# Cross-attention in a decoder layer: the eight PSUM banks dealt out anew, and the order of the projections, the mask and the input loads moved

## Chip, cores and metric

One core of a Trainium2 chip runs the whole kernel. The metric is the device time of one execution in microseconds (us). PE is TensorE, DVE is VectorE, ACT is ScalarE, POOL is GpSimd, SP is SyncE (it only issues DMAs here); PEld is the weight load of PE.

## What is computed

A decoder layer on x of shape (8, 512, 512): self-attention with 16 heads of 64, then cross-attention with 16 heads of 32 to a context of (8, 512, 384) with a key mask, then a quantised feed-forward; each with a layer norm in front and a residual. The change touches only the cross-attention:

```python
q = (x @ Wq) ...; k = (context @ Wk) ...; v = (context @ Wv) ...   # 16 heads of 32
scores = einsum('bhid,bhjd->bhij', q, k) * 32 ** -0.5
scores = where(context_mask[:, None, None, :], scores, max_neg)
out = einsum('bhij,bhjd->bhid', softmax(scores, -1), v)
return x + out @ Wo
```

## The kernel before

All of it is in `cross_attention_and_feed_forward_stage`, written by hand: each engine has its own instruction stream and waits on semaphores.

**Order.** The work goes by groups and slots. A group n is 4 heads of one batch element (4 groups to a batch element, N = 32 in all), and a slot is one tile of 128 keys by 512 queries of one head, so a group has U = 16 slots. Every engine walks the same list (G, s, t): G counts slots, s = G // 16 is the group whose scores are being made, t = G % 16. In slot G, PE issues, in this order: the scores of tile G-8 into bank `st` (`scores`, L2562), the maximum product of tile G+14 into `mx` (`max_scores`, L2544), at t = 3 the four transposes of the maxima into `ms` (`max_rows`, L2554), its share of the projections for group s+2, and the product with the values of tile G-12 into `ov` (`product`, L2572). Each product in float32 is made of parts: a value is split into a high and a low part, so a projection is three passes over its weights.

**Projections.** `KPASS` and `QPASS` (L1237) say how many matmuls of `key_projection` (9, L2514) and `query_projection` (12, L2525) a slot gets: keys 3 each in slots 0 to 2, queries 3 each in slots 3 to 6. Values (9 matmuls a tile, four tiles to a batch element) come in slots 7 to 10 and 12 to 15 of three groups out of four. A slot with a projection is called full here, one without is light. In the groups with s % 4 = 1 there are no values, but four tiles of context are transposed.

**Banks.** Keys go to `pj[:, 0]`, queries to `pj[:, 1]`, and every head's product goes to the one bank `ov`. `product` waits at the first tile of each head until ACT has copied the last head out (`out_rows`, L1918, which writes `osb`, first thing in its slot). Each key projection waits for `masked_key` of the group before, each query projection for `low_query` of the group before.

**Splitting.** DVE multiplies the keys by the mask (`masked_key`, L2105, in slot 3 behind the maximum and the two steps of the exponents), ACT takes the high part (`high_key`, slot 4), POOL the low part (`low_key`, slot 5). Queries: `high_query` on ACT in slot 7 (L1888), `low_query` on DVE in slot 8 (L2112). DVE also takes a maximum per slot (`maxima`, L2124) and half of the low parts of the exponents; POOL has the other half.

**SP.** It has no clock: it goes down its list and waits where a semaphore is not there yet. `stack_keys` and `stack_queries` (L1637, L1650; t = 8) send the seven 256 KB pieces of keys and queries to the tiles that PE reads; they wait for all scores of group n-3. `max_rows` (L1657, t = 5) sends the row of maxima that the first scores of the group need in slot 8. `outputs` (L1662, t = 1, 5, 9, 13) stores a head: `c_raw` (64 rows by 512, seen as 2 by 32 by 512) and `c_sums`. In groups with s % 4 = 1 there are also `load_sums` (L1670, t = 2, waits until all heads of the last batch element have landed; DVE takes their reciprocals in slot 5), `load_x` high (L1622, t = 7), `load_mask` (L1628, t = 9), `load_x` low (t = 9), and `store_reciprocals` (t = 10).

**Output projection.** From G = 474 on, `out_work` is mixed in every four slots, and goes on alone after the last slot. Its accumulators `acc` are `mx[:, 0]` and `pj[:, 1]`, its transposes `pt` go to `mx[:, 1]` and `ms`, and `spread_reciprocals` (L2612) writes `pj[:, 0]`.

Of the kernel before, what the change touches and what calls it, by code (L numbers as in the profile page):

```python
# [1215 lines left out]
def cross_attention_and_feed_forward_stage(nc, env):  # L1216
# [20 lines left out]
    KPASS, QPASS = (3, 3, 3), (0, 0, 0, 3, 3, 3, 3)  # L1237
# [33 lines left out]
    with ExitStack() as ctx:  # L1271
# [4 lines left out]
        with ExitStack() as life:  # L1276
# [51 lines left out]
            pj = bank("pj", [P, 2, S])  # L1328
            st = bank("st", [P, 2, S])
            mx = bank("mx", [P, 2, S])  # L1330
            ov = bank("ov", [P, S])
            ms = bank("ms", [P, S])
        dve_q = su.sem("dve_q")
# [197 lines left out]
        acc = lambda j: pj[:, 1] if j % 2 else mx[:, 0]  # L1531
        pt = lambda j: ms if j % 2 else mx[:, 1]
# [83 lines left out]
        def _(e):  # L1616
# [193 lines left out]
            for G, s, t in slots():  # L1810
                n = s + 2
                if t == 7 and s >= 0 and s % XG == 1 and s // XG + 1 < B:
                    load_x(s // XG + 1, 0)
                if t == 5 and 0 <= s < N:
                    max_rows(s)
                if t == 8 and n < N:
                    stack_keys(n)
                    stack_queries(n)
                if t == 1 and s >= 0 and s % XG == 0 and s // XG + 1 < B:
                    for i in range(NT):  # L1820
                        load_context(NT * (s // XG + 1) + i)
                if t % NT == 1 and 0 < s:
                    outputs(s - 1, t // NT)
                if t == 9 and s >= 0 and s % XG == 1 and s // XG + 1 < B:
                    load_mask(s // XG + 1)
# [50 lines left out]
        def _(e):  # L1876
# [11 lines left out]
            def high_query(n):  # L1888
                e.wait_ge(pe_q, n + 1)
                nc.scalar.activation(qh[:, :], pj[:, 1], ACT.Copy).then_inc(act_qh, 1)  # L1890
# [27 lines left out]
            def out_rows(n, j):  # L1918
# [3 lines left out]
                nc.scalar.activation(osb[:, j], ov[0:VW, :], ACT.Copy).then_inc(act_ov, 1)  # L1922
# [70 lines left out]
            for G, s, t in slots():  # L1993
# [21 lines left out]
                if t == 7 and n < N:  # L2015
                    high_query(n)
# [81 lines left out]
        def _(e):  # L2098
# [6 lines left out]
            def masked_key(n):  # L2105
# [4 lines left out]
                nc.vector.tensor_tensor(km[:, :], pj[:, 0], maskb[:, :], ALU.mult).then_inc(dve_km, 1)  # L2110

            def low_query(n):  # L2112
# [3 lines left out]
                nc.vector.tensor_tensor(ql[:, :], pj[:, 1], f32(qh[:, :]), ALU.subtract).then_inc(dve_ql, 1)  # L2116
# [78 lines left out]
            def out_work(i):  # L2195
# [17 lines left out]
                if is_chunk(n):  # L2213
                    e.wait_ge(pool_o, n + 1)
                    e.wait_ge(pe_rb, n + 1)
                    nc.vector.tensor_tensor(osum[:, n % SUM], osum[:, n % SUM], pj[:, 0], ALU.mult).then_inc(dve_o, 1)
# [28 lines left out]
            for G, s, t in slots():  # L2245
                n = s + 2
                m = G + U - LM - 1
                if 0 <= m < U * N:
                    maxima(m)
                if t == 11 and value_tile(s, 0) is not None:  # L2250
# [10 lines left out]
                if t == 3 and n < N:  # L2261
                    masked_key(n)
                if t == 8 and n < N:
# [228 lines left out]
        def _(e):  # L2492
# [21 lines left out]
            def key_projection(n):  # L2514
# [3 lines left out]
                if n:  # L2518
                    e.wait_ge(dve_km, n)
                for i, (w, part) in enumerate(((w_hi, 0), (w_lo, 0), (w_hi, 1))):  # L2520
                    for k in range(CK):
                        yield nc.tensor.matmul(pj[:, 0], w[:, k, cols(n % XG)], xc[:, part, k],  # L2522
                                               start=(i == 0 and k == 0), stop=(i == 2 and k == CK - 1))
# [297 lines left out]
```

## Time and profile before

| | us |
|---|---|
| median of 3 runs | 3456.7 |
| lowest, highest | 3453.31, 3459.38 |
| the profiled execution, its own time | 3453.76 |
| its span | 3452.1 |
| busy: PE, DVE, ACT, POOL | 3188.3, 2610.2, 2258.7, 1102.8 |
| cross-attention, first key projection to the end of the output projection | about 1544 to 2506 |

"Busy" of an engine counts its instructions; a matmul's duration overlaps the next one's start, so an engine can look busy through short waits. A wait stands in brackets behind the instruction that waited, with who released it. The DMA share is the mean over the 16 DMA engines. A window of the trace says, after its two ends: its length in us; the busy us of PE, PEld, DVE, ACT and POOL, each with its instructions in brackets; the granted PE clock as a share of full speed; the DMA share; GB/s, reads and writes together. The windows by batch element run from slot 3 of one s % 4 = 1 group to the next.

### The profile page before, as it was taken

Reading aid. Unit: us, or ns where it says so; the run is one execution under the profiler, and the core shown is the slowest. Engines: PE = TensorE matmul, PEld = TensorE weight load, DVE = VectorE, ACT = ScalarE, POOL = GpSimd, SP = SyncE. Lnnn points to the kernel's source line nnn. Section 1 sums busy time; section 2 is a strip of 40 time slices with the busy share of each in tenths; the row PEclk is TensorE's granted clock in tenths of the full one; section 3 lists DMA queues with packets and bytes.
Section 4 is the critical chain, followed back from the end, with each engine's and each line's share of the span. In section 5 each row is a group of like instructions: output and inputs, shape, how many; then the busy total and the mean of one; then the engine's idle time right before and its main releaser. Section 6 shows DMA issues by size and latency. Waiting matters only on the chain.

```text
span 3452.1 us, 47184 instructions
## 1 busy us (share of the span) xinstructions
PE 3188.3 (92%) x15056; PEld 2506.6 (73%) x15056; DVE 2610.2 (76%) x4327; ACT 2258.7 (65%) x4127; POOL 1102.8 (32%) x1192
## 2 busy tenths in 40 slices
PE   5999999999999999978999999988899999942998
PEld 4788888888888888865666666655678888731887
DVE  5987878787778777767888888887863479888564
ACT  4886767676766767655777777775442256578665
POOL 1233242333333333344666666666400000000000
PEclk9999999999999999989999999999999999975999
DMA  3453444444434433346656666555623268989764
GB/s 123 158 169 120 129 143 125 134 124 143 121 134 138 138 116 123 110 131 122 125 107 117 131 119 128 116 112 185 210 83 113 108 231 292 339 338 406 262 239 176
DMA packets 273028, 555.49 MB, mean 161 GB/s; under 512 B 28024, under 2 KB 105856, under 8 KB 259472
## 3 DMA queue, kind: packets, MB, share of 16 engines
q1 hardware_dynamic: 268560, 544.08, 52.6%
q10 hardware_dynamic: 4224, 8.39, 0.6%
q8 instruction: 124, 2.03, 0.2%
q14 instruction: 120, 0.98, 0.1%
HBM read 322.72 MB, written 162.30 MB: 141 GB/s over the span
## 4 chain that ended last, share of the span: by engine, by line
PE 37%; DMA 8%; DVE 5%; issue 2%; ACT 2%; SPq 1%; POOL 1%; POOLq 0%; ACTq 0%; DVEq 0%
PE gu_acc L2637 9%; PE ca_mx L2551 3%; PE ca_ov L2581 3%; PE md_acc L2723 3%; PE md_acc L2724 3%; PE md_acc L2725 3%; DMA ca_q<-ca_ql 2%; PE ca_ov L2582 2%; PE ca_st L2569 2%; PE ca_pj L2533 2%; PE ca_ms L2541 2%; PE ca_pj L2522 2%; DMA gu_g<-gate 1%; DMA gu_w_raw<-in_L_ffn_w_up_dram 1%; DMA md_ab<-up 1%
## 5 line engine op out<-in xcount | busy, mean ns | idle before, releaser
L915 POOL TENSOR_SCALAR sa_ex<-sa_ex,sa_rs 128x512 f32<-128x512 f32 x512 | 357.0, 697 | 906.6 <-DVE sa_rs L741 906.6
L736 DVE TENSOR_REDUCE sa_nm<-sa_st 128x1 f32<-128x512 f32 x512 | 350.3, 684 | 223.5 <-PE sa_st L1057 219.8
L578 ACT ACTIVATE sa_eh<-sa_tr 128x512 fp32r<-128x512 f32 x512 | 306.6, 599 | 293.5 <-PE sa_tr L1067 291.7
L1008 PE MATMUL sa_pj<-sa_xh,sa_w 128*128 128x512 f32 x1536 | 456.0, 416 | 3.0 <-DVE sa_xl L714 1.5
L2127 DVE TENSOR_REDUCE ca_negm<-ca_mx 128x1 fp32r<-128x512 f32 x512 | 345.0, 682 | 77.1 <-PE ca_mx L2551 74.8
L745 DVE TENSOR_TENSOR sa_el<-sa_tr,sa_eh 128x512 fp32r<-128x512 f32 x512 | 351.2, 686 | 41.0 <-ACT sa_eh L578 34.1
L571 ACT ACTIVATE sa_ex<-sa_st,sa_nm 128x512 f32<-128x512 f32 x512 | 351.3, 686 | 43.4 <-DVE sa_nm L736 39.5
L2420 POOL TENSOR_TENSOR ca_el<-ca_ex,ca_eh 128x512 fp32r<-128x512 f32 x256 | 359.9, 1411 | 40.0 <-ACT ca_eh L1916 39.1
L1908 ACT ACTIVATE ca_ex<-ca_st 128x512 f32<-128x512 f32 x512 | 298.5, 586 | 56.2 <-PE ca_st L2569 56.0
L1067 PE MATMUL sa_tr<-top_ident,sa_ex 128*128 128x128 f32 x2048 | 306.8, 272 | 1.9 <-POOL sa_ex L915 1.9
L1067 PEld LDWEIGHTS sa_tr<-top_ident,sa_ex 128*128 128x128 f32 x2048 | 254.3, 140 | 70.9 <-POOL sa_ex L915 4.3
L1008 PEld LDWEIGHTS sa_pj<-sa_xh,sa_w 128*128 128x128 f32 x1536 | 262.5, 190 | 40.5 <-issue 4.6
L1945 ACT ACTIVATE gu_ev<-gu_acc,top_x_scale 128x512 f32<-128x512 f32 x192 | 131.0, 683 | 203.7 <-PE gu_acc L2637 196.1
L1916 ACT ACTIVATE ca_eh<-ca_ex 128x512 fp32r<-128x512 f32 x320 | 201.3, 629 | 90.9 <-PE ca_ov L2582 86.8
L2142 DVE TENSOR_TENSOR ca_el<-ca_ex,ca_eh 128x512 fp32r<-128x512 f32 x256 | 247.4, 966 | 15.1 <-ACT ca_eh L1916 14.0
L2581 PE MATMUL ca_ov<-ca_eh,ca_vc 128*66 128x512 f32 x512 | 208.9, 408 | 27.3 <-ACT ca_osb L1922 22.7
L2551 PE MATMUL ca_mx<-ca_k,ca_q 97*128 97x512 f32 x512 | 212.3, 415 | 18.1 <-DMA ca_q<-ca_ql 14.3
L1008 PE MATMUL sa_pj<-sa_xl,sa_w 128*128 128x512 f32 x768 | 228.1, 405 | 0.0
L1078 PE MATMUL sa_ov<-sa_eh,sa_va 128*128 128x512 f32 x512 | 212.9, 416 | 4.2 <-DVE sa_el L745 3.6
L2569 PE MATMUL ca_st<-ca_q,ca_k 98*128 98x512 f32 x512 | 207.4, 405 | 5.8 <-DMA ca_q<-ca_mrow 5.8
L1056 PE MATMUL sa_st<-sa_ks,sa_qs 128*128 128x512 f32 x512 | 206.3, 403 | 0.0
L2582 PE MATMUL ca_ov<-ca_el,ca_vc 128*66 128x512 f32 x512 | 204.8, 400 | 0.0
(309 smaller groups left out, 7574.5 us busy)
## 6 DMA issues: line engine op xcount, KB each, us to landing
sa_w<-w_split SPq DMA_DIRECT2D x56, 1536.0 KB, 7.4
gate<-gu_ev SPq DMA_DIRECT2D x24, 1024.0 KB, 4.4
gu_g<-gate SPq DMA_DIRECT2D x48, 512.0 KB, 6.4
gate<-gu_g SPq DMA_DIRECT2D x48, 512.0 KB, 3.7
up<-gu_ev SPq DMA_DIRECT2D x24, 1024.0 KB, 5.7
md_ab<-gate SPq DMA_DIRECT2D x96, 256.0 KB, 6.5
md_ab<-up SPq DMA_DIRECT2D x96, 256.0 KB, 7.1
md_ab<-gate SPq DMA_DIRECT2D x44, 512.0 KB, 12.2
```

Of the source, the lines that this page charges most:

```text
L571: nc.scalar.activation(ex[:, u % U], st[:, u % 2], ACT.Exp, bias=nm[:, u % U:u % U + 1], accum_out=sums[:, u % U:u % U + 1]).then_inc(act_ ...
L578: nc.scalar.activation(eh[:, v % ER], tr[:, v % 2], ACT.Copy).then_inc(act_eh, 1)
L736: nc.vector.tensor_reduce(nm[:, u % U:u % U + 1], st[:, u % 2], AX_X, ALU.max, negate=True).then_inc(dve_mx, 1)
L745: nc.vector.tensor_tensor(el[:, v % ER], tr[:, v % 2], f32(eh[:, v % ER]), ALU.subtract).then_inc(dve_el, 1)
L915: nc.gpsimd.tensor_scalar(ex[:, u % U], ex[:, u % U], rs[:, u % U:u % U + 1], 1.0, ALU.mult, ALU.mult).then_inc(pool_n, 1)
L1008: yield nc.tensor.matmul(pj[:, bank], w[:, n % 2, m, part, k], xx[b % 2][:, k], start=(i == 0 and k == 0), stop=(i == 2 and k == DK - 1))
L1067: last = nc.tensor.transpose(tr[:, v % 2, rows(qt)], ex[:, (first + qt) % U, rows(kt)], ident[:, :])
L2127: nc.vector.tensor_reduce(negm[:, n % 2, qt, h:h + 1], mx[:, m % 2], AX_X, ALU.max, negate=True).then_inc(dve_mx, 1)
L2420: nc.gpsimd.tensor_tensor(el[:, a % EL], ex[:, a % EX], f32(eh[:, a % EL]), ALU.subtract).then_inc(low_done["pool"], 1)
L2551: nc.tensor.matmul(mx[:, m % 2], q4[0:MR + 1, r, h, cols(qt)], k4[0:MR + 1, r, h], start=True, stop=True).then_inc(pe_mx, 1)
L2581: nc.tensor.matmul(ov[0:VW, :], values, eh[:, a % EL], start=(kt == 0), stop=False)
L2637: last = nc.tensor.matmul(u_acc[:, a % BANKS], ww[:, k], xx[:, b, k], start=(n == 0 and k == 0), stop=(n == 2 and k == DK - 1))
```

## The change

It deals out the eight PSUM banks anew (`pj` one bank for keys, then queries; `ov` two banks, `ov[h % 2]`), and moves steps in the lists of PE, DVE, ACT and SP. Keys and queries now take turns in one bank: the query projection starts in slot 4 and waits for `masked_key` of its own group, the key projection waits for `low_query` of the group before. `product` waits for the head before last. `masked_key` stands right behind the maximum in slot 3.

```diff
-    KPASS, QPASS = (3, 3, 3), (0, 0, 0, 3, 3, 3, 3)
+    KPASS, QPASS = (3, 3, 3), (0, 0, 0, 0, 3, 3, 3, 3)
...
-            pj = bank("pj", [P, 2, S])
+            pj = bank("pj", [P, S])
+            ov0 = bank("ov0", [P, S])
             st = bank("st", [P, 2, S])
             mx = bank("mx", [P, 2, S])
-            ov = bank("ov", [P, S])
+            ov1 = bank("ov1", [P, S])
             ms = bank("ms", [P, S])
+            ov = (ov0, ov1)
...
-        acc = lambda j: pj[:, 1] if j % 2 else mx[:, 0]
-        pt = lambda j: ms if j % 2 else mx[:, 1]
+        acc = lambda j: ms[:, :] if j % 2 else mx[:, 0]
+        pt = lambda j: ov0 if j % 2 else mx[:, 1]
...
-                if t == 7 and s >= 0 and s % XG == 1 and s // XG + 1 < B:
+                if t == 10 and s >= 0 and s % XG == 1 and s // XG + 1 < B:
                     load_x(s // XG + 1, 0)
                 if t == 5 and 0 <= s < N:
                     max_rows(s)
                 if t == 8 and n < N:
                     stack_keys(n)
+                if t == 9 and n < N:
                     stack_queries(n)
+                if t == 4 and s >= 0 and s % XG == 1 and s // XG + 1 < B:
+                    load_mask(s // XG + 1)
...
-                if t == 9 and s >= 0 and s % XG == 1 and s // XG + 1 < B:
-                    load_mask(s // XG + 1)
+                if t == 12 and s >= 0 and s % XG == 1 and s // XG + 1 < B:
                     load_x(s // XG + 1, 1)
...
-                if t == 7 and n < N:
+                if t == 8 and n < N:
                     high_query(n)
...
+                if t == 3 and n < N:
+                    masked_key(n)
...
-                if t == 3 and n < N:
-                    masked_key(n)
-                if t == 8 and n < N:
+                if t == 9 and n < N:
                     low_query(n)
...
             def key_projection(n):
                 if n:
-                    e.wait_ge(dve_km, n)
+                    e.wait_ge(dve_ql, n)
...
             def query_projection(n):
-                if n:
-                    e.wait_ge(dve_ql, n)
+                e.wait_ge(dve_km, n + 1)
...
             def product(a):
                 if kt == 0:
                     e.wait_ge(dve_vl, NT * b + NT)
-                    if a:
-                        e.wait_ge(act_ov, a // NT)
+                    if a >= 2 * NT:
+                        e.wait_ge(act_ov, a // NT - 1)
-                nc.tensor.matmul(ov[0:VW, :], values, eh[:, a % EL], start=(kt == 0), stop=False)
+                nc.tensor.matmul(ov[h % 2][0:VW, :], values, eh[:, a % EL], start=(kt == 0), stop=False)
...
-                    if t == 3:
+                    if t == 4:
                         work["q"] = query_projection(n)
```

In the output projection, tile 1 now waits for `ms` (`bank_free`) at its product, and for the last head in `ov0` at its transposes; `spread_reciprocals` and the DVE step behind it use all of `pj`.

## Rows read from the trace of the kernel before

**Rows 1.** Windows: length; busy PE, PEld, DVE, ACT, POOL; clock; DMA share; GB/s.
```profile
1698.56:1796.71 98.15, 94.45 (x405) 66.20 (x404) 81.56 (x123) 75.34 (x142) 60.11 (x53) 0.98 0.63 121
...
1893.43:1988.99 95.56, 92.89 (x405) 65.18 (x404) 82.12 (x123) 75.00 (x142) 60.45 (x53) 1.00 0.64 124
...
2183.24:2281.87 98.63, 94.97 (x405) 66.20 (x404) 82.73 (x123) 75.41 (x142) 60.09 (x53) 0.98 0.60 112
```
**Rows 2.** Waits of PE, 1698.56 to 2281.87: who for whom, us in total, times, longest.
```profile
PE ca_ov L2581 <- ACT ca_osb L1922: 8.9, 20, 0.9
PE ca_st L2569 <- DMA ca_q<-ca_mrow: 5.8, 5, 1.8
PE ca_mx L2551 <- DMA ca_q<-ca_ql: 3.9, 5, 1.6
```
**Rows 3.** Groups of instructions of the page (section 5), DVE's two costly ones.
```profile
L2127 DVE TENSOR_REDUCE ca_negm<-ca_mx 128x1 fp32r<-128x512 f32 x512 | 345.0, 682 | 77.1 <-PE ca_mx L2551 74.8
L2142 DVE TENSOR_TENSOR ca_el<-ca_ex,ca_eh 128x512 fp32r<-128x512 f32 x256 | 247.4, 966 | 15.1 <-ACT ca_eh L1916 14.0
```
**Rows 4.** Timeline of PE: start, us, instruction.
```profile
1996.93 0.40 PE L2569 MATMUL ca_st<-ca_q,ca_k 98*128 98x512 f32 x1
...
2004.29 0.40 PE L2569 MATMUL ca_st<-ca_q,ca_k 98*128 98x512 f32 x1
...
2005.25 0.39 PE L2569 MATMUL ca_st<-ca_q,ca_k 98*128 98x512 f32 x1
...
2012.91 0.50 PE L2551 MATMUL ca_mx<-ca_k,ca_q 97*128 97x512 f32 x1 [1.64 <-DMA ca_q<-ca_ql]
```
**Rows 5.** Windows of 1 us: first group, three of the fastest batch element, the slowest.
```profile
1604.00:1605.00 1.00, 1.00 (x6) 0.73 (x5) 1.00 (x3) 1.00 (x3) 0.46 (x1) 1.00 0.00 0
...
1913.00:1914.00 1.00, 1.00 (x6) 0.71 (x5) 1.00 (x2) 0.90 (x3) 1.00 (x1) 1.00 1.03 203
...
1949.00:1950.00 1.00, 1.00 (x6) 0.78 (x5) 0.86 (x2) 1.00 (x3) 1.00 (x1) 1.00 0.10 31
1966.00:1967.00 1.00, 1.00 (x7) 0.72 (x6) 1.00 (x3) 0.61 (x2) 0.80 (x1) 1.00 0.13 49
...
2237.00:2238.00 1.00, 1.00 (x6) 0.81 (x5) 0.66 (x2) 1.00 (x3) 0.06 (x1) 1.00 0.03 10
```
**Rows 6.** The chain that ended last, 2060 to 2100: start, us, what.
```profile
2077.43 11.83 DMA c_sums<-ca_osb
2089.39 2.54 DMA ca_sums<-c_sums
2091.96 0.55 DVE ca_rec L2149
```
**Rows 7.** Timeline of SP (DMA issues): start, us to issue.
```profile
1992.38 0.66 SPq L1659 DMA_DIRECT2D ca_q<-ca_mrow  x1
...
1995.40 0.58 SPq L1625 DMA_DIRECT2D ca_xq<-xn_hi  x1
...
2000.65 0.75 SPq L1634 DMA_DIRECT2D ca_q<-ca_ql  x1
```
**Rows 8.** The mask tile: its DMAs from issue to landing.
```profile
DMA to landing us min/median/max: 3.2/11.7/12.4
```
**Rows 9.** Timeline of DVE around a masked key with s % 4 = 2.
```profile
2207.51 0.94 DVE L2142 TENSOR_TENSOR ca_el<-ca_ex,ca_eh 128x512 fp32r<-128x512 f32 x1
2209.23 0.69 DVE L2110 TENSOR_TENSOR ca_km<-ca_pj,ca_maskb 128x512 f32<-128x512 f32 x1 [0.79 <-issue]
```
**Rows 10.** Timeline of PE in the same group: the query pass of slot 4.
```profile
2210.26 0.40 PE L2533 MATMUL ca_pj<-ca_xq,ca_w_hi 128*128 128x512 f32 x1
```
**Rows 11.** Window behind the 1.80 us wait of 2217.60.
```profile
2217.60:2225.00 7.40, 7.40 (x25) 5.24 (x26) 5.20 (x7) 4.54 (x9) 3.58 (x3) 0.77 1.07 142
```
**Rows 12.** Waits, 2308 to 2400, and the longest one of ACT before them.
```profile
PE ca_ov L2581 <- ACT ca_osb L1922: 11.1, 11, 6.5
...
ACT ca_wo_hi L1968 <- DMA ca_xn<-in_L_xattn_Wo_dram: 8.4, 1, 8.4
```

More of the change, by code:

```diff
@@ L1889, in high_query @@
                 e.wait_ge(pe_q, n + 1)
-                nc.scalar.activation(qh[:, :], pj[:, 1], ACT.Copy).then_inc(act_qh, 1)
+                nc.scalar.activation(qh[:, :], pj[:, :], ACT.Copy).then_inc(act_qh, 1)
             def high_value(j):
@@ L1921, in out_rows @@
                     e.wait_ge(o_out[j], 32 * n)
-                nc.scalar.activation(osb[:, j], ov[0:VW, :], ACT.Copy).then_inc(act_ov, 1)
+                nc.scalar.activation(osb[:, j], ov[j % 2][0:VW, :], ACT.Copy).then_inc(act_ov, 1)
             def high_reciprocals(b):
@@ L2109, in masked_key @@
                     e.wait_ge(pool_kl, n)
-                nc.vector.tensor_tensor(km[:, :], pj[:, 0], maskb[:, :], ALU.mult).then_inc(dve_km, 1)
+                nc.vector.tensor_tensor(km[:, :], pj[:, :], maskb[:, :], ALU.mult).then_inc(dve_km, 1)
             def low_query(n):
@@ L2115, in low_query @@
                     e.wait_ge(stacked[(n - 1) % RING], STACKS * ((n - 1) // RING) + STACKS)
-                nc.vector.tensor_tensor(ql[:, :], pj[:, 1], f32(qh[:, :]), ALU.subtract).then_inc(dve_ql, 1)
+                nc.vector.tensor_tensor(ql[:, :], pj[:, :], f32(qh[:, :]), ALU.subtract).then_inc(dve_ql, 1)
             def low_value(j):
@@ L2215, in out_work @@
                     e.wait_ge(pe_rb, n + 1)
-                    nc.vector.tensor_tensor(osum[:, n % SUM], osum[:, n % SUM], pj[:, 0], ALU.mult).then_inc(dve_o, 1)
+                    nc.vector.tensor_tensor(osum[:, n % SUM], osum[:, n % SUM], pj[:, :], ALU.mult).then_inc(dve_o, 1)
                 j = i - 1
@@ L2518, in key_projection @@
                 if n:
-                    e.wait_ge(dve_km, n)
+                    e.wait_ge(dve_ql, n)
                 for i, (w, part) in enumerate(((w_hi, 0), (w_lo, 0), (w_hi, 1))):
                     for k in range(CK):
-                        yield nc.tensor.matmul(pj[:, 0], w[:, k, cols(n % XG)], xc[:, part, k],
+                        yield nc.tensor.matmul(pj[:, :], w[:, k, cols(n % XG)], xc[:, part, k],
                                                start=(i == 0 and k == 0), stop=(i == 2 and k == CK - 1))
@@ L2532, in query_projection @@
                     for k in range(DK):
-                        yield nc.tensor.matmul(pj[:, 1], w[:, 2 * CK + k, cols(g)], xq[:, part, k],
+                        yield nc.tensor.matmul(pj[:, :], w[:, 2 * CK + k, cols(g)], xq[:, part, k],
                                                start=(i == 0 and k == 0), stop=(i == 2 and k == DK - 1))
@@ L2577, in product @@
                     e.wait_ge(dve_vl, NT * b + NT)
-                    if a:
-                        e.wait_ge(act_ov, a // NT)
+                    if a >= 2 * NT:
+                        e.wait_ge(act_ov, a // NT - 1)
                 values = vc[b % 2][:, kt, HS * g + h]
-                nc.tensor.matmul(ov[0:VW, :], values, eh[:, a % EL], start=(kt == 0), stop=False)
-                nc.tensor.matmul(ov[0:VW, :], values, el[:, a % EL], start=False, stop=(kt == NT - 1)).then_inc(pe_av, 1)
+                nc.tensor.matmul(ov[h % 2][0:VW, :], values, eh[:, a % EL], start=(kt == 0), stop=False)
+                nc.tensor.matmul(ov[h % 2][0:VW, :], values, el[:, a % EL], start=False, stop=(kt == NT - 1)).then_inc(pe_av, 1)
             def out_product(i):
@@ L2588, in out_product @@
                     e.wait_ge(dve_mx, U * N)
+                if i == 1:
+                    bank_free()
                 if i >= 2:
@@ L2606, in out_transposes @@
                 elif j == 1:
-                    bank_free()
+                    e.wait_ge(act_ov, HS * N - 1)
                 for k in range(DK):
@@ L2618, in spread_reciprocals @@
                     e.wait_ge(dve_ql, N)
-                nc.tensor.matmul(pj[:, 0], cast_r[:, :], rc[:, n % 2], start=True, stop=True).then_inc(pe_rb, 1)
+                nc.tensor.matmul(pj[:, :], cast_r[:, :], rc[:, n % 2], start=True, stop=True).then_inc(pe_rb, 1)
             def u_transposes(i):
```

## The prediction

> **What bounds the kernel now.** I read the windows by batch element first. A batch element is four groups, 64 slots; the six from 1698.56 to 2281.87 take 583.3 us, 97.2 each, between 95.56 and 98.63 for the same instructions [rows 1]. The reader is to see two things: PE is busy 93 of 96 us in the fastest, so little can be had from PE; and they differ by 3 us with nothing different to compute, so something else holds them.
>
> Next the waits of PE [rows 2]. In six batch elements it waited 8.9 us for ACT to empty the bank of the last head (20 times, 0.45 on average), 3.9 for the last piece of the stacked queries, 5.8 for the row of maxima. In sum 18.6, 3.1 per batch element. Waits under about 0.16 do not show, since a matmul's 0.39 outlasts its pitch of 0.23 (a light slot of four matmuls: 2004.29 to 2005.25, 0.96) [rows 4].
>
> Third, who else is full. In a light slot DVE owes a maximum, 0.68, and half a low part, 0.97 / 2 = 0.48 [rows 3]: 1.16 at least against PE's 0.96. So light stretches go at DVE's pace already, and a wait of PE inside one is partly time it would have waited anyway.
>
> Last, the DMA engines, and here I see the bound. In 96 windows of 1 us over the fastest batch element the share is near 1 while the seven stack pieces run, and otherwise about 0.13; it never falls below 0.10 [rows 5]. 0.13 of 16 engines is two engines. Between the bursts exactly two are busy, without a hole, and the stores of the heads are what SP issues then. The two slowest batch elements have holes (0.03 at 2237). The chain agrees: a store of sums took 11.83 us to land, SP could not load the sums before, and DVE stood until the load had landed, 2.54 more [rows 6]. Once per batch element everything queued on those two engines has to be through.
>
> The Trainium skill, "DMA: Bandwidth & Descriptors", section on why a DMA increments its semaphore by 16, says that a DMA runs on the largest number of engines up to 16 that divides the slowest dimension of both sides, and on the lowest-numbered ones. By that rule a store seen as 2 by 32 by 512 runs on two engines, always the same; the share of 0.13 agrees.
>
> **Two banks for the heads.** This takes away the wait for `out_rows`. Ceiling: 8.9 us in six batch elements, 1.5 each, and a hidden 0.16 for each of 16 heads, 2.5. Floor: nothing, where DVE is late next. ACT's copies and their number stay. In steady state what remains is set by the two engines, below.
>
> **One bank for keys and queries.** No matmul is added. The query passes move from slots 3 to 6 to slots 4 to 7. Slot 3 keeps the four transposes and gets light, slot 7 gets full (six matmuls where values start too). PE's sum is the same, and DVE gains a full slot before the light ones: between 0 and 0.5 us per batch element, part of the next sum.
> The new wait for the masked key: in the tightest kind of group the key was masked from 2209.23 to 2209.92, after 0.79 us of a wait that is not named, which I read as the mask not landed [rows 9]. The new first query pass would stand where slot 4's pass is, less the 0.7 us that slot 3 loses: 2210.26 - 0.7 = 2209.6 [rows 10]. With the mask there early and the key ahead of the low part (0.94), it ends near 2208.8, 0.8 us ahead. Bounds: 0 per group, and 0.3 (2209.92 less 2209.6) if the mask were still late; I take 0. Behind `masked_key` on DVE stand two exponent steps, late by 0.68, which the full slot 4 covers; without cover POOL's and PE's next product would wait 0.68. The key projection's new wait is for a step of slot 9, seven slots earlier: 0.
> `high_query` and `low_query` come a slot later, 1 to 1.6 us. The queue hides it, because the four key pieces go out first and keep all engines busy. At the very start of the stage nothing hides it: +1 us once, at most 2.
>
> **The loads.** The high half of x (1 MB, issued 1995.40) goes behind the stack pieces instead of ahead, and `ql` (issued 2000.65, waited for until 2012.91 [rows 4, 7]) lands earlier by what 1 MB takes. At the 203 GB/s of the burst [rows 5] that is 5 us, or 10 if reads and writes share the figure; both are over the longest wait, 1.6. The 3.9 us go: 0.65 per batch element. But the row of maxima, two groups of stores later, waits for all of it in any order, so this wait moves to it. The low half of x is needed three slots after the high half and still lands before two stores that stand ahead of that row: 0.
> The mask (256 KB) leaves the burst for a quiet time: 1/16 of the 4 MB that are sent from 1995.40 on. Of the 17.5 us to 2012.91 that is 1.1; as the two engines have stores besides, I take half, 0.5 us less for the row of maxima; bounds 0 and 1.1. It now stands ahead of the row of maxima of the s % 4 = 1 group: issue 0.35, and data. That row is issued 1992.38 and needed 1996.93, 4.55 later [rows 4, 7]. Bounds: 0 and 3.2, a mask's shortest landing [rows 8]; I take 0.5, as most of 3.2 is latency that overlaps.
>
> **The sum, steady state.** PE's way gets shorter by up to 1.5 + 0.65 + 0.5, some 2.6 us per batch element; the mask gives 0.5 and takes 0.5. The two engines have the same bytes to move. They were full for 95.6 us in the fastest batch element, and holes are all that can be closed: 97.2 to some 96.4. So 0.8 in each of six, 5 us; the other 1.8 comes back as longer waits for the row of maxima and for the sums. **Before 1698** the engines have holes (a share of 0.00 at 1604 [rows 5]), so PE sets the pace and most of one batch element's 2.6 is won: -2, with the +1 at the start -1. **After 2308**: 11.1 us of waits for the head's bank, of which 6.5 lie behind ACT's 8.4 us wait for an output weight [rows 12], which blocks the exponents too and stays; of the other 4.6 I take half, as DVE and POOL are near full: -2. The banks of the output projection: 0. In all -8 us: the profiled execution 3453.76 to 3446, and, as it lies 2.9 below the median, 3449 against 3456.7; I say 3448.
>
> **Rivals.**
> *A. The two engines keep the pace* (above): 3448, own range 3442 to 3454. For it: a share that never falls under two engines. Against: that could be chance, with a backlog that just happens not to run out. Chance 0.45.
> *B. PE's waits set the pace.* Then 8.9 and 3.9 and 2 of the 5.8 are won in six batch elements, 14.8; as much per batch element before 1698, 2.5; 4.6 at the end: 22 us, 3435. For it: PE is 97% busy (92.89 of 95.56). Against: rows 1 and 6. Chance 0.22.
> *C. The banks' wait is only replaced by DVE's, no gain:* 3456. For it: 1.16 against 0.96 per light slot. Chance 0.13.
> *D. Slower: the mask ahead of the row of maxima.* It decides if that row takes over 4.55 us to land. With 2 us in each of seven batch elements, +14, less 5 of the rest: +9, 3466. A pause of 1.80 us also left PE at a granted clock of 0.77 for 7.4 us, which is 1.7 us lost [rows 11]; part of these would come on top. Chance 0.20.
> The Trainium skill, "DMA: Bandwidth & Descriptors", section "Queues, rings and completion order", says that each engine consumes its ring in order. By that a small row waits for the mask's packets ahead of it; it speaks for D, and no run here shows its price yet.
>
> **The numbers.** A measurement can tell about 0.2%, 7 us, from no change. Of A somewhat more than half lies beyond it (0.27), with all of B (0.22) and a bit of C: faster 0.51. Same: the rest of A and C and a little of D, 0.31. Slower 0.18. The range takes in B and nearly D: 3431 to 3465.
>
> **What would show it.** Right: no wait of PE for `ca_osb` of 0.3 to 0.9 between 1698 and 2281; no wait for `ca_ql` in s % 4 = 2; longer waits for `ca_mrow` and of SP for `c_sums`; batch elements of 96 to 97 us, the DMA share never under 0.10. If batch elements fall to 94, the two engines were no bound and I am wrong towards B. Waits for `ca_mrow` in s % 4 = 1 show D; waits of PE for `ca_km` would show the bank for keys and queries too tight.

## The result, and the profile after

| | before | after |
|---|---|---|
| median of 19 runs each, us | 3454.7 (3446.74 to 3465.61) | 3462.01 (3458.65 to 3468.17) |
| span of the profiled execution, us | 3452.1 | 3460.7 |

The ratio is 1.0018, with a 95% interval of 1.0011 to 1.0024. The changed kernel is slower by 0.18%. That is small, but the interval lies wholly on the slower side, where the forecast of 3448 had it faster.

The page of the changed kernel: the span, the row of busy times, and four groups of section 5. Where the head's product had waited for ACT, PE now waits for the row of maxima and for the maximum of DVE.

```profile
span 3460.7 us, 47184 instructions
...
PE 3188.3 (92%) x15056; PEld 2508.9 (72%) x15056; DVE 2616.6 (76%) x4327; ACT 2253.6 (65%) x4127; POOL 1097.9 (32%) x1192
...
L2131 DVE TENSOR_REDUCE ca_negm<-ca_mx 128x1 fp32r<-128x512 f32 x512 | 342.9, 680 | 85.5 <-PE ca_mx L2554 83.1
...
L2146 DVE TENSOR_TENSOR ca_el<-ca_ex,ca_eh 128x512 fp32r<-128x512 f32 x256 | 240.2, 938 | 17.5 <-ACT ca_eh L1920 16.4
L2554 PE MATMUL ca_mx<-ca_k,ca_q 97*128 97x512 f32 x512 | 213.4, 417 | 20.8 <-DVE ca_negm L2131 9.7
...
L2572 PE MATMUL ca_st<-ca_q,ca_k 98*128 98x512 f32 x512 | 209.2, 409 | 19.6 <-DMA ca_q<-ca_mrow 13.4
```

The waits of PE in the six batch elements, 1698.91 to 2290.11, the lines that answer to [rows 2]:

```profile
PE ca_st L2572 <- DMA ca_q<-ca_mrow: 11.8, 6, 2.1
PE ca_mx L2554 <- DVE ca_negm L2131: 7.1, 18, 0.5
PE ca_pj L2536 <- DMA ca_xq<-xn_hi: 3.8, 6, 0.8
PE ca_ms L2514 <- DVE ca_xc L2106: 1.5, 6, 0.3
```

The waits for `ca_osb` (8.9 us) and `ca_ql` (3.9) are gone, as meant. The one for the row of maxima doubled, from 5.8 to 11.8, and falls in every batch element; two are new, for DVE's maximum (before: 1.2) and for the high half of x.

Windows of the changed kernel by batch element, columns as in [rows 1]; three of the six; the first takes 97.44, the other five 98.65 to 98.97:

```profile
1698.91:1796.35 97.44, 93.12 (x405) 65.51 (x404) 83.05 (x123) 74.95 (x142) 60.05 (x53) 1.00 0.65 121
...
1895.00:1993.65 98.65, 94.39 (x405) 66.61 (x404) 83.58 (x123) 75.00 (x142) 59.56 (x53) 0.98 0.65 120
...
2191.43:2290.11 98.68, 94.45 (x405) 66.61 (x404) 83.34 (x123) 75.02 (x142) 59.38 (x53) 0.98 0.63 112
```

The six take 591.2 us against 583.3: +7.9. With +0.35 ahead of them (1698.91 against 1698.56) and +0.35 behind (+1.1 in the tail of the table below, -0.7 in the feed-forward), that is the 8.6 by which the spans differ. So the question is what happens inside a batch element, and there one cuts further: from slot 3 of each group (its transposes) to slot 3 of the next. The same batch element of the changed kernel in four windows, for the steps from s % 4 = 1 to 2, 2 to 3, 3 to 0 and 0 to 1:

```profile
1895.00:1918.67 23.67, 22.78 (x103) 15.52 (x102) 21.13 (x35) 19.41 (x39) 15.16 (x14) 1.00 0.78 149
1918.67:1945.36 26.69, 24.19 (x99) 17.07 (x98) 20.64 (x30) 18.54 (x35) 14.46 (x14) 0.94 0.58 121
1945.36:1969.59 24.23, 24.23 (x108) 18.01 (x107) 20.76 (x31) 18.78 (x36) 14.91 (x14) 1.00 0.68 116
1969.59:1993.65 24.06, 23.20 (x99) 16.00 (x98) 21.05 (x30) 18.26 (x35) 15.02 (x14) 1.00 0.57 93
```

and of the kernel before, its fastest batch element:

```profile
1893.43:1917.88 24.45, 23.16 (x102) 15.30 (x101) 20.33 (x35) 19.54 (x39) 15.55 (x14) 1.00 0.73 184
1917.88:1941.42 23.54, 22.64 (x100) 16.06 (x99) 20.85 (x30) 18.19 (x35) 14.94 (x13) 1.00 0.57 95
1941.42:1965.71 24.29, 24.29 (x109) 17.91 (x108) 20.90 (x31) 18.92 (x36) 14.85 (x14) 1.00 0.68 119
1965.71:1988.99 23.28, 22.81 (x99) 15.91 (x98) 20.03 (x30) 18.34 (x35) 15.10 (x14) 1.00 0.58 95
```

Summed over the six batch elements, for every kernel of this study (us; the tail runs from slot 3 of the last batch element's s % 4 = 1 group to the first matmul of the feed-forward):

| kernel | 1 to 2 | 2 to 3 | 3 to 0 | 0 to 1 | sum | tail |
|---|---|---|---|---|---|---|
| before | 151.1 | 146.3 | 145.9 | 140.0 | 583.3 | 224.3 |
| after | 142.0 | 159.4 | 145.5 | 144.3 | 591.2 | 225.4 |
| after_late | 143.3 | 149.0 | 145.5 | 144.3 | 582.0 | 232.6 |
| before_late | 179.8 | 144.7 | 146.1 | 139.9 | 610.5 | 235.7 |
| after_split | 142.0 | 139.9 | 145.5 | 144.3 | 571.6 | 219.4 |
| before_split | 151.1 | 141.2 | 145.9 | 140.2 | 578.4 | 216.8 |
| after_x7 | 162.5 | 141.7 | 145.5 | 144.2 | 593.9 | 222.1 |
| after_mask9 | 142.1 | 161.7 | 145.5 | 144.3 | 593.6 | 226.9 |
| as_onebank | 142.0 | 139.3 | 145.6 | 139.6 | 566.4 | 218.4 |
| as_kmlast | 143.5 | 140.7 | 146.8 | 145.6 | 576.5 | 218.6 |
| after_onebank | 142.6 | 157.2 | 148.0 | 139.4 | 587.2 | 221.9 |
| as_pause | 141.9 | 139.5 | 145.5 | 139.3 | 566.2 | 217.4 |
| bs_loads | 144.3 | 145.8 | 146.0 | 140.4 | 576.4 | 221.5 |
| after_fill | 142.0 | 153.3 | 145.5 | 144.3 | 585.0 | 224.5 |

The first two lines say it: the change wins 9.1 in the first step and loses 13.1 in the second and 4.3 in the fourth. The first loss holds the waits for the row of maxima (6.0 more) and for x (3.8). A third part shows in the windows right behind the wait for the row of maxima. Two of these waits in the timeline of PE of the changed kernel:

```profile
1732.75 0.50 PE L2572 MATMUL ca_st<-ca_q,ca_k 98*128 98x512 f32 x1 [1.82 <-DMA ca_q<-ca_mrow]
...
2027.61 0.50 PE L2572 MATMUL ca_st<-ca_q,ca_k 98*128 98x512 f32 x1 [2.06 <-DMA ca_q<-ca_mrow]
```

and the windows that begin at the ends of the first four:

```profile
1732.75:1740.00 7.25, 7.23 (x30) 4.89 (x30) 6.48 (x10) 5.89 (x11) 3.57 (x3) 1.00 1.09 148
1830.14:1838.00 7.86, 7.86 (x27) 5.58 (x28) 6.17 (x9) 5.49 (x11) 3.58 (x3) 0.78 1.09 146
1928.80:1936.00 7.20, 7.20 (x24) 5.05 (x25) 5.63 (x9) 4.81 (x9) 3.36 (x3) 0.76 1.07 147
2027.61:2035.00 7.39, 7.39 (x25) 5.24 (x26) 5.99 (x9) 4.89 (x10) 3.19 (x3) 0.77 1.08 151
```

Behind the pause of 1.82 us PE kept its full clock; behind the next three it ran at a mean of 0.76 to 0.78 of full speed, a mix of its two levels, 1.2 and 2.4 GHz. Of the six only the first batch element is spared, and it is the one of 97.44: 1.2 us shorter, of which 0.2 is its shorter wait. In the trace of the kernel before, the windows behind the waits of 1.65 and 1.80 us for the row of maxima stand at 0.77, those behind 1.41 and 0.73, and behind the 1.64 for the queries [rows 4], at 1.00: two falls there, five here. The three more, at 1.2 (the price that `after_fill` shows below), are about the rest of the 13.1 (6.0 + 3.8 + 3.7 = 13.5).

### The profile page after: what moved, and what is told of

It is laid out like the page before. It is cut to its first block, busy times and chain, and to the rows that moved or that the text cites. A ratio compares the mean times of both kernels' runs of the same rounds, so it can differ in the third digit from the quotient of the medians.

```text
span 3460.7 us, 47184 instructions
## 1 busy us (share of the span) xinstructions
PE 3188.3 (92%) x15056; PEld 2508.9 (72%) x15056; DVE 2616.6 (76%) x4327; ACT 2253.6 (65%) x4127; POOL 1097.9 (32%) x1192
## 4 chain that ended last, share of the span: by engine, by line
PE 34%; DVE 8%; DMA 8%; issue 2%; ACT 2%; SPq 1%; POOL 1%; ACTq 0%; POOLq 0%; DVEq 0%
PE gu_acc L2642 7%; PE ca_mx L2554 3%; PE md_acc L2728 3%; PE md_acc L2729 3%; PE md_acc L2730 3%; PE ca_st L2572 2%; PE ca_ov L2585 2%; PE ca_ov L2584 2%; DMA gu_g<-gate 2%; PE ca_pj L2536 2%; PE ca_pj L2526 2%; PE ca_ms L2544 2%; DMA ca_q<-ca_mrow 2%; DVE ca_negm L2131 1%; DMA gu_w_raw<-in_L_ffn_w_up_dram 1%
## 5 line engine op out<-in xcount | busy, mean ns | idle before, releaser
L2146 DVE TENSOR_TENSOR ca_el<-ca_ex,ca_eh 128x512 fp32r<-128x512 f32 x256 | 240.2, 938 | 17.5 <-ACT ca_eh L1920 16.4
```

## The experiments

Labels that begin with `after` or `before` change that kernel; `as_` stands on `after_split`, `bs_` on `before_split`. Each batch of runs has its own runs of the kernel before beside it, so kernels of different batches are compared by their ratios to it.

### Later stores: after_late, before_late

The first head's store goes behind the row of maxima.

```diff
-                if t % NT == 1 and 0 < s:
-                    outputs(s - 1, t // NT)
+                if t in (5, 6, 9, 13) and 0 < s:
+                    outputs(s - 1, 0 if t == 6 else t // NT)
```

> The changed kernel with one store moved: the first head's store (and sums) of the group before goes out in slot 6, behind the row of maxima, instead of in slot 1 ahead of it. Nothing is left out. Theory T1 (the row of maxima queues behind the stores of heads, which only two DMA engines carry; the pause of 2.05 us also costs PE its full clock): the row waits for two stores instead of three, so PE's wait for it, 2.05 us at s % 4 = 2, falls below 0.3, its clock stays at 1.00 in the window behind it, batch elements fall from 98.7 to about 96, and the kernel gains 12 to 20 us on the changed one. Theory T2 (the row waits for the x loads and stack pieces on all sixteen engines, whatever the stores do): the wait stays at 1.8 to 2.1 us and the time within 3 us. Theory T3 (the loss of the change comes from DVE, which falls behind in the light slots): waits for the row matter little, under 5 us gained.

> The same single move of one store in the kernel before. T1: its waits for the row (5 in six batch elements, 5.8 us) go, those for the queries (3.9) stay or grow a little; 3 to 8 us faster than before. T2 and T3: the same time within 3 us.

Measured: `after_late` 3465.66 us, ratio 1.0031 (1.002 to 1.0042). The wait for the row of maxima is gone, the one for the high half of x is 7.7 us in place of 3.8, and the batch elements take 97.0 instead of 98.5 on average. But the tail grew by 7.2 us, so in sum nothing was won, and the 12 to 20 us that T1 had expected did not come. In the tail, PE's waits for the reciprocals that the output projection loads (`ca_rc`) grew from 7.9 to 14.1 us; that the late stores make them is argued, not shown. What the run shows is that the row of maxima was late because of what SP sends ahead of it: with one head's store (and its sums) behind it the wait is gone.

`before_late` 3496.43 us, ratio 1.0118 (1.0104 to 1.0133), where T1 had it 3 to 8 us faster and the other two theories the same. Its wait for a DMA in 1698 to 2290:

```profile
PE ca_mx L2551 <- DMA ca_q<-ca_ql: 23.7, 6, 5.0
```

In the kernel before, the stack pieces follow slot 8 and their last one is the tight transfer (3.9 us of waits [rows 2]); a store in slot 6 stands right ahead of them. The wait is the measurement; that the store's place makes it was not tried apart.

### Two engines or sixteen: after_split, before_split

The store of a head, seen as 2 by 32 by 512, is issued as two of 32 by 512. The counts that are waited for on its semaphore go from 32 to 48 with it (not shown).

```diff
-                e.dma_start(c_raw[g, :, j * XD:(j + 1) * XD, at], osb[0:2 * XD, j]).then_inc(o_out[j], 16)
+                for q in range(2):
+                    e.dma_start(c_raw[g, q, j * XD:(j + 1) * XD, at], osb[q * XD:(q + 1) * XD, j]).then_inc(o_out[j], 16)
```

> The changed kernel with each head's store of 2 by 32 rows sent as two DMAs of 32 rows, so that by T1 sixteen engines carry it and no longer two; nothing else changes, SP issues 128 DMAs more (0.5 us each). T1: the share of 0.13 between bursts goes, waits for the row of maxima and for the high half of x vanish or fall under 0.3, PE's clock stays at 1.00, batch elements fall to 94 to 95.5, the kernel gains 20 to 35 us on the changed one. T2: the same bytes take as long, within 3 us. T3: under 5 us gained, since DVE's waits (7.1 us in six batch elements) stay.

> The kernel before with the same split stores. T1: its DMA waits (9.7 us in six batch elements, and SP's for the sums) go and only the waits for the head's bank stay (8.9): batch elements of about 95.5, 10 to 20 us faster than before, and now slower than the changed kernel with split stores, as rival B of the prediction had it, by 5 to 15 us. T2: no change. T3: the change itself costs some 6 us with split stores too, so before_split is faster than after_split.

Measured: `after_split` 3433.4 us, ratio 0.994 (0.9928 to 0.9951), which is 0.8% below the changed kernel. `before_split` 3443.11 us, 0.9969 (0.9957 to 0.9982). A window of 1 us of `after_split`, and one of the changed kernel, the lowest of its batch element:

```profile
1916.00:1917.00 1.00, 1.00 (x6) 0.78 (x5) 1.00 (x1) 0.70 (x2) 0.62 (x1) 1.00 0.00 0
```

```profile
1948.00:1949.00 1.00, 1.00 (x6) 0.77 (x5) 1.00 (x3) 1.00 (x3) 0.60 (x1) 1.00 0.03 8
```

Of the 96 windows of a batch element 13 are at 0.00 with the split store, and of the changed kernel's only two lie below 0.10. The shelf at 0.13 was the old store on two engines. The waits of PE in `after_split`, 1698 to 2290, hold no DMA any more:

```profile
PE ca_mx L2555 <- DVE ca_negm L2132: 7.3, 19, 0.5
PE ca_st L2573 <- ACT ca_ex L1913: 2.0, 7, 0.3
PE ca_ov L2585 <- POOL ca_el L2425: 1.8, 2, 1.6
PE ca_ms L2515 <- DVE ca_xc L2107: 1.5, 6, 0.3
```

and those of `before_split` still hold both old ones:

```profile
PE ca_ov L2582 <- ACT ca_osb L1923: 14.4, 25, 0.9
PE ca_mx L2552 <- DMA ca_q<-ca_ql: 4.0, 4, 1.8
PE ca_mx L2552 <- DVE ca_negm L2128: 1.0, 6, 0.2
```

So the two engines were the bound for the row of maxima and for x. They were not what made `ca_ql` late, and they did not set the pace of the whole batch element either: against the changed kernel 18 of the 24 steps are unchanged, and only the step 2 to 3 fell, from 159.4 to 139.9.

### The places of the loads: after_x7, after_mask9, bs_loads

`after_x7` puts the halves of x back to slots 7 and 9, `after_mask9` the mask back to slot 9, `bs_loads` gives `before_split` all three new places and nothing else.

```diff
-                if t == 10 and s >= 0 and s % XG == 1 and s // XG + 1 < B:
+                if t == 7 and s >= 0 and s % XG == 1 and s // XG + 1 < B:
                     load_x(s // XG + 1, 0)
...
-                if t == 12 and s >= 0 and s % XG == 1 and s // XG + 1 < B:
+                if t == 9 and s >= 0 and s % XG == 1 and s // XG + 1 < B:
                     load_x(s // XG + 1, 1)
```

```diff
-                if t == 4 and s >= 0 and s % XG == 1 and s // XG + 1 < B:
+                if t == 9 and s >= 0 and s % XG == 1 and s // XG + 1 < B:
                     load_mask(s // XG + 1)
```

```diff
+                if t == 4 and s >= 0 and s % XG == 1 and s // XG + 1 < B:
+                    load_mask(s // XG + 1)
-                if t == 7 and s >= 0 and s % XG == 1 and s // XG + 1 < B:
+                if t == 10 and s >= 0 and s % XG == 1 and s // XG + 1 < B:
                     load_x(s // XG + 1, 0)
...
-                if t == 9 and s >= 0 and s % XG == 1 and s // XG + 1 < B:
-                    load_mask(s // XG + 1)
+                if t == 12 and s >= 0 and s % XG == 1 and s // XG + 1 < B:
                     load_x(s // XG + 1, 1)
```

> The changed kernel with both loads of x back in their old slots, 7 and 9 (the mask stays early). T1, by which the row of maxima at s % 4 = 2 waits for everything queued on two engines in whatever order: its wait of 2.05 us stays within 0.5, or shrinks by what a returning wait for the queries (0.5 to 1.6) takes off it; the wait for the high half of x (0.5 to 0.8) goes; batch elements of 97.5 to 99, the kernel within 6 us of the changed one. T4 (the moved loads of x are what put the bytes in front of the row): its wait falls under 0.7, PE's clock stays full, 8 us or more faster than the changed kernel, at or below the kernel before.

> The changed kernel with the mask's load back in slot 9. Rival D of the prediction, that the mask ahead of the row of maxima costs: 6 us or more faster than the changed kernel. T1: no wait for the row at s % 4 = 1 is there to remove, so no gain; the mask is in the burst again, lands as late as slot 3 of the next group, and now the query projection waits behind the masked key: a wait of 0.5 to 2 us in one group of four, the same time or up to 8 us slower.

> The kernel before with split stores and only the loads moved as in the change (mask in slot 4, x in slots 10 and 12). It tells what of the 16 us between it and the one-bank version comes from the loads, and what from the passes. If the loads matter: no wait for the queries (4.0 us in six batch elements) and none for the mask, batch elements of 95.4 to 95.6 from the start on, 4 to 8 us faster than without. The rest of the way to 94.4 per batch element, some 7 us, is then the passes moved to slots 4 to 7. If the loads don't matter, the time is within 3 us of the one with split stores alone.

Measured: `after_x7` 3467.88 us, ratio 1.0036 (1.0023 to 1.005). Its waits for DMAs in 1698 to 2290 are one line:

```profile
PE ca_mx L2554 <- DMA ca_q<-ca_ql: 13.8, 6, 3.1
```

The loads' new places do what they should (without them, the last piece of the queries is late by 13.8 us in place of 0), and take 3.8 for x and 11.8 for the row in return. A wait moved; its sum stayed near 15. The kernel before, with the same places for x, waited only 3.9 for that piece; there the queries are sent a slot earlier, but which part of the change makes the difference was not tried apart.

`after_mask9` 3465.82 us, 1.0022 (1.0012 to 1.0032); waits for DMAs:

```profile
PE ca_st L2572 <- DMA ca_q<-ca_mrow: 12.2, 6, 2.1
PE ca_pj L2536 <- DMA ca_xq<-xn_hi: 9.4, 6, 1.6
```

The row of maxima is not earlier with the mask out of its way, and x is later. Rival D, the mask ahead of the row, falls. The expected wait for the masked key did not show either; the longer wait is put down to x. The trace holds one thing more. All six waits for the row are 1.92 to 2.07 us long, and behind four of them PE kept its full clock; this is the window behind one of 2.06 us:

```profile
2031.90:2039.00 7.10, 7.09 (x29) 4.89 (x30) 6.32 (x9) 5.87 (x11) 3.57 (x3) 1.00 1.08 148
```

With two falls for five, 5.6 more for x and 0.4 more for the row, the six batch elements should take 2.4 us more than the changed kernel's at 1.2 a fall (5.6 + 0.4 - 3.6), and they do (593.6 against 591.2).

`bs_loads` 3442.06 us, 0.9959 (0.9946 to 0.9972), against 0.9969 without the moved loads: nothing that can be told apart. The wait for `ca_ql` (4.0) is gone, 3.0 us of waits for `xn_hi` have come. The step 1 to 2 wins 6.8, the step 2 to 3 gives back 4.6 and the tail 4.7.

### One head bank again: as_onebank, after_onebank

Every product in `ov1`, with the old wait for the last head; all else as changed. The same edit on `after_split` and on the changed kernel; ACT's copy reads `ov[1]` with it (not shown).

```diff
-                    if a >= 2 * NT:
-                        e.wait_ge(act_ov, a // NT - 1)
+                    if a:
+                        e.wait_ge(act_ov, a // NT)
-                nc.tensor.matmul(ov[h % 2][0:VW, :], values, eh[:, a % EL], start=(kt == 0), stop=False)
+                nc.tensor.matmul(ov[1][0:VW, :], values, eh[:, a % EL], start=(kt == 0), stop=False)
```

> The changed kernel with split stores, and the heads' products back in one bank (the other is left for the transposes of the output projection). The DMA waits are away here, so this is the worth of the second bank by itself. Theory P (the waits for the head's bank were PE's own time): the intervals between groups grow by 0.3 to 0.9 each, 1.5 to 2.5 per batch element of 95.2, and the kernel loses 12 to 20 us. Theory C (DVE's pace in the light slots takes the place of that wait): batch elements within 0.8 us, the kernel within 6 us; the interval from s % 4 = 0 may even go back from 24.05 towards the 23.3 of before.

> The changed kernel, stores as they are, with the heads' products back in one bank. The split runs showed that the second bank costs 0.8 us per batch element, in the interval from s % 4 = 0 (24.05 against 23.26). If only PE and DVE counted, the kernel would gain 5 to 8 us on the changed one. Theory T1 (the two DMA engines of the stores hold the batch element): PE arrives 0.8 us earlier at the row of maxima and waits as much longer for it, and for the high half of x: batch elements within 0.5 us of 98.6, the kernel within 4 us of the changed one.

Measured: `as_onebank` 3426.83 us, ratio 0.9915 (0.9901 to 0.9928), the lowest median of the study, 0.25% below `after_split`. Neither theory had it: P expected a loss, and C at most 6 us. Waits of PE in 1698 to 2290:

```profile
PE ca_ov L2585 <- ACT ca_osb L1927: 14.3, 26, 5.5
PE ca_ov L2585 <- POOL ca_el L2425: 1.9, 2, 1.6
```

It waits 14.3 us for the head's bank, and is faster. The second bank costs time, 4.7 us in the step 0 to 1 (144.3 against 139.6). The place is in the light slots of that step. DVE's low parts (L2147) alone, in this step, as a window with busy time and clock, of `after_split`:

```profile
1957.87:1981.92 24.05, 8.04 (x9) 1.00 0.60 91
```

and of `as_onebank`:

```profile
1955.51:1978.77 23.26, 6.91 (x9) 1.00 0.62 94
```

Nine of the same instructions take 1.13 us more. The timeline shows which. In `after_split`, DVE's timeline and below it POOL's:

```profile
1973.62 1.12 DVE L2147 TENSOR_TENSOR ca_el<-ca_ex,ca_eh 128x512 fp32r<-128x512 f32 x1
1974.66 1.27 DVE L2132 TENSOR_REDUCE ca_negm<-ca_mx 128x1 fp32r<-128x512 f32 x2
1975.86 1.82 DVE L2147 TENSOR_TENSOR ca_el<-ca_ex,ca_eh 128x512 fp32r<-128x512 f32 x1
...
1973.58 0.62 POOL L2418 TENSOR_SCALAR ca_eh<-ca_ex 128x512 fp32r<-128x512 f32 x1 [0.77 <-ACT ca_ex L1913]
1974.16 2.96 POOL L2425 TENSOR_TENSOR ca_el<-ca_ex,ca_eh 128x512 fp32r<-128x512 f32 x2
```

in `as_onebank` the same slots:

```profile
1971.28 0.68 DVE L2147 TENSOR_TENSOR ca_el<-ca_ex,ca_eh 128x512 fp32r<-128x512 f32 x1
1971.88 1.27 DVE L2132 TENSOR_REDUCE ca_negm<-ca_mx 128x1 fp32r<-128x512 f32 x2
1973.07 1.17 DVE L2147 TENSOR_TENSOR ca_el<-ca_ex,ca_eh 128x512 fp32r<-128x512 f32 x1
...
1971.62 0.81 POOL L2418 TENSOR_SCALAR ca_eh<-ca_ex 128x512 fp32r<-128x512 f32 x1 [1.15 <-ACT ca_ex L1913]
1972.40 2.99 POOL L2425 TENSOR_TENSOR ca_el<-ca_ex,ca_eh 128x512 fp32r<-128x512 f32 x2
```

In both, POOL makes a high part (L2418) and then a pair of low parts, 3 us long. In these rows the step that starts second is the one that gets longer. With two banks DVE's subtraction starts at 1973.62, just behind POOL's high part (1973.58), and takes 1.12 for 0.68; with one bank it starts ahead of it (1971.28 against 1971.62), takes 0.68, and POOL's high part takes 0.81 for 0.62. The second subtraction meets the pair in both: it takes 1.17 with one bank, and 1.82 with two, where it starts 0.02 behind the second low part of the pair (1975.84 in a narrower view). The next maxima are late, and PE waits 0.3 to 0.4 for `ca_negm` twice in this step and never gets it back: some 4 of the 7 us of these waits in six batch elements. `as_onebank` has none of them there. Over the six batch elements DVE's low parts, 193 in each trace, take 180.1 us in `after_split` and 173.4 in `as_onebank`.

`after_onebank` 3453.01 us, ratio 0.9986 (0.9975 to 0.9997), against 1.0018 for the changed kernel: some 0.3%, 11 us, more than was expected. The step 0 to 1 gives 4.9 of it, the tail 3.5. The step 2 to 3 gives 2.2 and the step 3 to 0 takes 2.5. That last one alternates between 24.26 and 25.07 us, and DVE's nine low parts in it between 7.04 and 8.34: the same effect in another place. So T1 falls in the form that it has here, by which the two engines hold the batch element and the kernel stays within 4 us.

### A pause in one place: as_pause

If it is only the standing of PE to POOL in these slots that counts, one wait per batch element must do. The two banks stay; the product of the first head of each s % 4 = 0 group waits as in the kernel before.

```diff
-                    if a >= 2 * NT:
+                    if a and h == 0 and n % XG == 0:
+                        e.wait_ge(act_ov, a // NT)
+                    elif a >= 2 * NT:
                         e.wait_ge(act_ov, a // NT - 1)
```

> The changed kernel with split stores, two banks, and the old wait for the last head's copy put back for one head in sixteen: the first of a group with s % 4 = 0, whose product stands in slot 12. Theory R (that pause of 0.46 us lets DVE's subtraction get ahead of POOL's pair, 0.68 instead of 1.12 us and 1.17 instead of 1.82): the interval from s % 4 = 0 goes from 24.05 to 23.3, batch elements from 95.2 to 94.4, the kernel gains 4 to 8 us, like the kernel with one bank. Theory S (something else about the two banks, such as which bank PE writes while ACT reads): the interval stays at 24.0 or above and the time the same.

Measured: 3429.51 us, ratio 0.9925 (0.9912 to 0.9939). The step 0 to 1 takes 139.3 instead of 144.3, the batch elements 566.2 in sum, as with one bank, and DVE's low parts 173.1 us in place of 180.1. A wait of PE added, 5 us won in the profile. The times of `as_pause` and `as_onebank` cannot be told apart.

### The masked key: as_kmlast

`masked_key` back behind the two exponent steps of slot 3.

```diff
-                if t == 3 and n < N:
-                    masked_key(n)
...
+                if t == 3 and n < N:
+                    masked_key(n)
                 if t == 9 and n < N:
                     low_query(n)
```

> The changed kernel with split stores, and the masked key back behind the two exponent steps of slot 3. Prediction's step: the masked key ended 0.8 us ahead of the query pass because it went ahead of a step of 0.7 to 0.9; without that PE waits 0 to 0.3 us for the masked key in each of 32 groups, up to 5 us slower than with it ahead. If the earlier key is what delays DVE's exponents and costs the 0.75 us in the interval from s % 4 = 0, that interval goes back to 23.3 and the kernel gains about 5 us.

Measured: 3438.26 us, ratio 0.995 (0.9937 to 0.9962), against 0.994: 0.1%, which the times alone do not tell apart, and in the profile 4.9 us over the six batch elements, about 0.2 in each of the 24 steps. PE has no wait for the masked key here, so its place was not needed for the queries to start in time. What grew is the time of DVE's low parts, from 180.1 to 194.6 us: with the later key more of them meet a step of POOL. That the key's first place pays is shown by the profile; that it pays by this is likely from that sum, and was not tried apart.

### Six matmuls in the pause: after_fill

Six matmuls whose result nobody reads go into `ms` ahead of the wait for the late row of maxima.

```diff
+                if t == LA and s % XG == 2 and 0 < s < N - 2:
+                    bank_free()
+                    for _ in range(6):
+                        nc.tensor.matmul(ms[:, :], w_hi[:, 0, cols(0)], xc[:, 0, 0], start=True, stop=True)
```

> The changed kernel with six idle matmuls (1.4 us) ahead of the first scores of groups with s % 4 = 2, in the 2.05 us in which PE waits for the row of maxima; they write a bank that is free then and is written anew before it is read. Theory K (a pause of over 1.8 us costs PE its full clock for some 7 us, 1.2 us of time): the wait is 0.6 at most, the window behind it shows a clock of 1.00, the interval from s % 4 = 2 goes from 26.7 to 25.5, and the kernel gains 4 to 8 us. If the clock's fall costs nothing that the DMA engines do not already cost, the interval stays and the time is within 3 us.

Measured: 3458.35 us, ratio 1.0006 (0.9998 to 1.0015), against 1.0018 (1.0011 to 1.0024): some 4 us, with intervals that overlap. The row is still late, but PE now waits 0.4 to 0.7 for it, and the step 2 to 3 of the same batch element is:

```profile
1918.86:1944.25 25.39, 24.30 (x106) 17.11 (x104) 20.47 (x30) 18.53 (x35) 15.11 (x14) 1.00 0.61 124
```

Clock 1.00 for 0.94, 25.39 us for 26.69, with the six matmuls in the window. Over the six batch elements of the profile 6.2 us are won, five falls at 1.2, and the only thing taken away is PE's idleness. The granted clock of the whole executions agrees: a mean of 0.9698 over the 12 of this kernel, 0.9681 over the 19 of the changed one.

## Why the prediction was wrong

**Right: the engines behind the 0.13 shelf.** The store of a head ran on two DMA engines and made the row of maxima late; `after_split` shows both, and `after_late` shows the second by itself. The Trainium skill, "DMA: Bandwidth & Descriptors", section on why a DMA increments its semaphore by 16, agrees with it: cut so that the slowest dimension is 32, the same bytes leave windows at 0.00.

**Right: what goes and what comes.** No wait for `ca_osb`, none for `ca_ql`, longer ones for the row of maxima; the mask cost nothing (`after_mask9`), and neither did the wait for the masked key. (The prediction's 2208.8 for the end of the masked key does not come out of its rows, 2209.92 less 0.79 and 0.94 is 2208.2; the 0 that it stood for held.)

**Wrong, first: "the other 1.8 comes back as longer waits for the row of maxima".** It came back, gathered in one pause of 1.8 to 2.1 us per batch element, and I had priced a pause by its length alone. Behind five of six the clock fell, 1.2 us each; before, behind two. I had the row for it [rows 11], priced it at 1.7 where it measured 1.2, and used it only for rival D; it belongs to A as soon as A makes that wait longer. `after_fill` shows about 6 us of it in the profile.

**Wrong, second: "Two banks. Floor: nothing".** The floor was below nothing. The second bank cost 4.7 us in the step 0 to 1 over six batch elements, because DVE's subtractions then start behind POOL's steps, and in the step 1 to 2, where most of the waits for the bank had stood, it won nothing (142.0 with either). The bound "nothing, where DVE is late next" took DVE's step at 0.97 / 2 wherever it stands; 0.97 is a mean of 0.68 and of some 1.1 to 1.8. This is rival C with another sign; three runs show it (`as_onebank`, `as_pause`, `after_onebank`).

**Wrong, third: "the low half of x ... 0".** Not the low half, but the high half was late, 0.63 in each batch element, 3.8 in all.

**The size.** -5 was forecast for the six batch elements and +7.9 measured. By step: -9.1 (with split stores 6.8 of it come with the loads, `bs_loads`, and 1.5 with the masked key, `as_kmlast`), +13.1 (row of maxima +6.0, x +3.8, the rest, 3.3, three more falls of the clock), -0.4, +4.3 (the second bank). The -1 before them measured +0.35, and the -2 behind them +1.1 in the tail.

**The two engines did not set the pace of everything.** I read "the share never falls under 0.10" as a floor of 95.6 per batch element. They set the time of one transfer: the split stores changed one step of four, and `after_onebank`, with the old stores, won 4.0 us in the six batch elements, which A would have returned as waits. Under split stores a batch element takes 95.3 (`after_split`) and 94.4 (`as_onebank`). With the old stores none is under 95.56 in any trace here, so how low they would let it go stays open. The sum of rival B, 22 us, has a near match: with split stores, the change's other parts (passes, loads, masked key) take `before_split`, 0.9969, to `as_onebank`, 0.9915, 0.5% or some 18 us, about 5 of them the masked key's. But that is not B's mechanism, since `as_onebank` still waits 14.3 us for the head's bank, the wait that B priced highest.

**The best version** is `as_onebank`: the change without its second head bank, with stores of 32 rows: 3426.83 us, 0.85% below the kernel before. `as_pause`, at 0.9925, is as good within the intervals.

**Open:** whether the late stores make the longer tail of `after_late`, what exactly made `before_late` slow, and why pauses of 1.82 and of 1.92 to 2.07 us left the clock alone where others of 1.65 to 2.06 did not.

## What to carry to other kernels

A wait removed from the busiest engine moves everything behind it: price the wait that takes its place, and also what the new standing does to engines that slow each other down, for half a microsecond of wait can be cheaper than two steps side by side. When a steady, low share of the DMA engines shows between bursts, look at the shape of the transfers that run then before any order is changed. And cost a longer pause of PE with the clock that goes with it, from the window behind such a pause.

## What was not expected of the hardware

- **DVE beside POOL.** A subtraction of two 128x512 fp32 tiles takes DVE 0.68 us alone or where it starts first, and 1.12 to 1.82 where it starts behind a step of POOL on its own tiles; where DVE was first, POOL's step took 0.81 for 0.62. DVE's maxima beside it keep their 0.68 (1.27 for two). The Trainium skill, "SBUF — State Buffer", section "Who interferes with whom", says that a DVE instruction with two SBUF inputs contends with a GpSimd instruction that reads SBUF, and that a reduction does not. The traces agree on both.
- **A DMA cut in two is faster than one.** 0.8% on the changed kernel, 0.3% on the one before, for one issue more of some 0.5 us on SP. The Trainium skill, "DMA: Bandwidth & Descriptors", section "Rules for kernel authors", advises against two transfers for two halves, since both would go over all 16 engines anyway. Where the one transfer runs on two engines, as here, the measurement is the other way.
- **The clock falls behind short pauses, and not by their length alone.** 1.65, 1.80 and 1.84 us idle, then 0.77 to 0.78 over the next 7 to 8 us; 1.82 us idle, and four times 1.92 to 2.07 in `after_mask9`, then 1.00. With six matmuls for nobody (1.3 us of work, by the wait that went from 2.04 to 0.71) it stayed at 1.00 behind all six waits.
